# Fourteen constant matmuls between routing and experts, and the down matmuls of block 6 ahead of the up matmuls of block 8

## The chip, the cores and the metric

One core of one Trainium2 chip runs the whole program. The metric is the device time in microseconds of one execution. TensorE (PE in the profile) does the matmuls, VectorE (DVE) and ScalarE (ACT) the elementwise work, GpSimd (POOL) some elementwise work and the indirect transfers, and SyncE (SP) issues nearly all other transfers. A profile is one execution taken by the hardware profiler; the times of the runs are taken without it.

## What is computed

The input `x` is 1024 tokens of 128 features, the context 6404 rows of 128. Cut to what matters:

```python
def xattn(c, q):                      # c = layernorm(x), q = context
    s = (c @ w_c + b_c)[:, :, None] + (q @ w_q + b_q)[:, None, :] + einsum('bcd,bqd,d->bcq', c, q, w_cq) + b_cq
    c2q = softmax(s, axis=2) @ q
    q2c = softmax(max(s, axis=2)) @ c
    return concat([c, c2q, c * c2q, c * q2c]) @ W_l.T + b_l
def ffn(x):                           # 8 experts, H 128, F 512, top 1
    expert_id = argmax(x @ wr + br)
    y_e = gelu(x @ w1[e] + b1[e]) @ w2[e] + b2[e]
    return y of the chosen expert
x = x + xattn(layernorm(x), ctx)
x = x + ffn(layernorm(x))
```

## The kernel before, in words

The first part (to about 171 us of the profiled span) is the attention: eight tiles of 128 tokens against seven groups of 1024 context rows, in f16 pairs of a high and a low part. The change lies behind it.

Then comes routing. On TensorE: `turn_x2` transposes the normalised rows of tiles 0 to 6, `router` makes their scores, `linear_a(3)` and `linear_c(2)` finish the attention's linear layer of tile 7, and the matmuls of L1210 to L1217 count ranks within each expert once VectorE has the one-hot choices (`chosen_ready`). VectorE turns the counts into positions (`pos_ready`, L955), finishes the layernorm of tile 7 (L760), and L1221 transposes that tile. ScalarE and VectorE split the transpose into high and low parts (L690, L964, `x7T_low`), for which the first expert matmuls wait.

The experts work in blocks. `NBLK` is 22: blocks 0 to 7 (`b < E`) put tile 7 through each of the eight experts with a mask; blocks 8 to 21 are dispatched blocks, up to 128 rows each that chose the same expert. For every block `up(b)` is 16 matmuls of 128 columns (L1265 to L1268, four per piece of the hidden layer), ScalarE takes the gelu twice (L708, L709), VectorE makes the low part of the hidden values (L983, `h_low`), and `down(b)` is four matmuls of 256 columns (L1279), one with the bias (L1282), then behind a wait for `h_low` four of 128 columns (L1285). VectorE finishes the block in two halves (L992 or L996, then L1006 or L1008, `y_ready`). Buffers for hidden values and results are a ring of three blocks. TensorE's order is written out by hand: in iteration `b` it runs `up(b + 2)` and then `down(b)`.

Dispatched rows take a way through device memory. After `pos_ready` GpSimd scatters the rows of seven tiles into `rows_by_expert` (L600, seven indirect transfers). SyncE waits for all of them (`rows_sent`) and then loads the rows of batches of 3, 4, 4 and 3 blocks (L447, `rows_landed`), in one queue with the fourteen copies of each block's weights (L442, `fetch`, 512 KB each). TensorE's `turn(g)` (L1239) transposes batch g in float32; ScalarE (L698) and VectorE (L975, `xT_low`) split it into two f16 parts. `turn(0)` stands at the head of iteration 6, `turn(1)` in iteration 6 behind `up(8)`, `turn(2)` in iteration 10 and `turn(3)` in iteration 14. `up(8)` waits for `xT_low` of batch 0. Blocks 8 to 21 leave by one indirect scatter each on GpSimd (L606), in order, each behind its `y_ready`. With the last of them landed the program ends.

`psS` is three PSUM tiles of two banks each. `psS[2][:, 0:512]` holds the transposes of `turn_a(0)` and of `turn_x2`'s first group earlier, and `up(2)` writes it later. `ones` is a float32 tile of ones.

Of the kernel before, what the change touches and what calls it, by code (L numbers as in the profile page):

```python
# [24 lines left out]
F16 = mybir.dt.float16  # L25
# [5 lines left out]
P = 128  # L31


def build(nc, x, ctxT, w3, b3, wlT, b_l, wr, br, w1, b1, w2, b2, out):
    N, D = x.shape
    Q = ctxT.shape[1]
    E, _, F = w1.shape
    T = N // P
    QT = -(-Q // P)
    QP = QT * P  # L40
    FC = F // P
    CH = 512
# [32 lines left out]
    def tiles(e):  # L75

        return range(e * TW, min((e + 1) * TW, QT))

    es = ExitStack()
    with es:  # L80
        def sb(name, shape, dt=F32):
            return es.enter_context(nc.sbuf_tensor(name, shape, dt))
# [24 lines left out]
        ones = sb("ones", [P, P])  # L107
# [88 lines left out]
        psS = [es.enter_context(nc.psum_tensor(f"psS{i}", [P, GR], F32)) for i in range(BANKS)]  # L196
# [126 lines left out]
        def rows_of(n):  # L323

            k = len(tiles(n))
            buf = qT[:, n, :, :] if n < NG - 1 else qTend[:, :, :]
            return buf.rearrange("p a w -> p (a w)"), qn[:, 2 * n * TW:2 * n * TW + 2 * k, :]
# [38 lines left out]
        def _(sp):  # L366
# [18 lines left out]
            def transpose(t, e):  # L385

                wait_low(sp, t, e)
                if t > 0:
                    sp.wait_ge(pv_done, (t - 1) * NG + e + 1)
                src, _, _, dst = piece(t, e)  # L390
                sp.dma_start_transpose(dst, src).then_inc(pT_landed[e], 16)
# [636 lines left out]
        def _(pe):  # L1028
# [30 lines left out]
            def weighted(t, e):  # L1059

                pe.wait_ge(pT_landed[e], 16 * (t + 1))
                if t == 0:
                    pe.wait_ge(qn_landed[e], 16)
                if t == 0 and e == 0:
                    pe.wait_ge(cT_ready, 1)
                if t == 1 and e == 0:
                    pe.wait_ge(row_term_ready, 1)
                if e == 0 and t > 1:
                    pe.wait_ge(o_out, t - 1)
                n, acc = len(tiles(e)), psA[t % 2]  # L1070
                both = rows_of(e)[1].rearrange("p (a j) d -> p a j d", a=2)
                for i, j in enumerate(tiles(e)):
                    nc.tensor.matmul(acc[:, 0:2 * D].rearrange("p (a d) -> p a d", a=2), PT[:, 2 * e * TW + i, :],  # L1073
                                     both[:, :, i, :], start=(j == 0), stop=False, skip_group_check=True)
                    last = nc.tensor.matmul(acc[:, 0:D], PT[:, 2 * e * TW + n + i, :], both[:, 0, i, :],  # L1075
                                            start=False, stop=(j == QT - 1), skip_group_check=True)
                last.then_inc(pv_done, 1)
# [43 lines left out]
            def linear_a(g):  # L1121

                t0, t1 = TURNS[g]
                pe.wait_ge(caT_ready, g + 1)
                if g < 2:
                    pe.wait_ge(nM_ready, 1)
                pe.wait_ge(late_landed, 16 * NLATE)
                for t in range(t0, t1):
                    k = t // H if t < T - 1 else 2
                    dst = z_psum[k][:, (t - GROUPS[k][0]) * D:(t - GROUPS[k][0] + 1) * D]  # L1130
                    r = slice(t * P, (t + 1) * P)
                    nc.tensor.matmul(dst, aT[:, r], wl[:, 1, :], start=(t == GROUPS[k][0]), stop=False,
                                     skip_group_check=True)
                    nc.tensor.matmul(dst, caT[:, r], wl[:, 2, :], start=False, stop=False, skip_group_check=True)

            def linear_c(g):

                t0, t1 = GROUPS[g]
                pe.wait_ge(wc2_ready, 1)
                for t in range(t0, t1):  # L1140
                    last = nc.tensor.matmul(z_psum[g][:, (t - t0) * D:(t - t0 + 1) * D], cT[:, t * P:(t + 1) * P],
                                            wc2[:, :], start=False, stop=(t == t1 - 1), skip_group_check=True)
                last.then_inc(z_in_psum, 1)
# [26 lines left out]
            def mean_context():  # L1170

                pe.wait_ge(eb_ready, 1)
                for t in range(T):
# [2 lines left out]
                nc.tensor.matmul(psS[1][:, CH:CH + 1], ones[:, :], es1[:, :], start=True, stop=True)\  # L1176
                    .then_inc(q2c_in_psum, 1)

            weighted(T - 2, 2)
            pe.wait_ge(scores_out, T * NG)  # L1180
            turn_a(0)
# [19 lines left out]
            for e in range(2, NG):  # L1201
# [3 lines left out]
            router()  # L1205
            linear_a(3)
            linear_c(2)

            pe.wait_ge(chosen_ready, 1)
            nc.tensor.matmul(rank_psum, before[:, :], oneh[:, :, :].rearrange("p t e -> p (t e)"),  # L1210
                             start=True, stop=False, skip_group_check=True)
            for t in range(TA - 1):
                nc.tensor.matmul(rank_psum[:, (t + 1) * E:TA * E], ones16[:, :],
                                 oneh[:, t, :].unsqueeze(1).broadcast_to([P, TA - 1 - t, E]),
                                 start=False, stop=(t == TA - 2), skip_group_check=True)
            for t in range(TA):
                last = nc.tensor.matmul(count_psum, ones16[:, :], oneh[:, t, :], start=(t == 0), stop=(t == TA - 1))  # L1217
            last.then_inc(ranks_in_psum, 1)

            pe.wait_ge(x2n_ready, H + 1)  # L1220
            nc.tensor.transpose(x7T_psum, x2n[:, TA, :], idf[:, :]).then_inc(x7T_in_psum, 1)  # L1221
# [8 lines left out]
            def turn(g):  # L1230

                s0, s1 = BATCHES[g]
                pe.wait_ge(rows_landed[g], 16)
                if g == 0:
                    pe.wait_ge(mask_ready, 1)
                if g >= 2:
                    pe.wait_ge(xT_low, g - 1)
                for b in range(s0, s1):
                    last = nc.tensor.transpose(psXT[g % 2][:, (b - s0) * P:(b - s0 + 1) * P], rows[:, b, 0:D], idf[:, :])  # L1239
                last.then_inc(xT_in_psum, 1)  # L1240

            def weights(b):

                return wp[:, :, b * F:(b + 1) * F] if b < E else block_w(b - E)

            def bias_rows(b):

                return pick[:, b, :] if b < E else chosen[:, b - E:b - E + 1].broadcast_to([P, P])

            def up(b):  # L1250

                i, j = b % RING, b - E if b >= E else NB
                if b >= E:
                    g = [s0 <= j < s1 for s0, s1 in BATCHES].index(True)
                    pe.wait_ge(xT_low, g + 1)
                    pe.wait_ge(block_w_landed[j % WSLOTS], 16 * (j // WSLOTS + 1))
                    pe.wait_ge(chosen_rows, 1)
                else:
                    pe.wait_ge(x7T_low, 1)
                if b >= RING:  # L1260
                    pe.wait_ge(h_full, b - RING + 1)
                for f in range(FC):
                    dst = psH[i][:, f * P:(f + 1) * P]
                    w_h, w_l = (weights(b)[:, a, f * P:(f + 1) * P] for a in range(2))
                    nc.tensor.matmul(dst, w_h, xTp[:, 0, j, :], start=True, stop=False)  # L1265
                    nc.tensor.matmul(dst, w_h, xTp[:, 1, j, :], start=False, stop=False)
                    nc.tensor.matmul(dst, w_l, xTp[:, 0, j, :], start=False, stop=False)
                    last = nc.tensor.matmul(dst, b12[:, f * P:(f + 1) * P],  # L1268
                                            bias_rows(b), start=False, stop=True)
                last.then_inc(h_in_psum, 1)  # L1270

            def down(b):

                i = b % RING
                if b >= RING:
                    pe.wait_ge(y_ready, b - RING + 1)
                pe.wait_ge(h_high, b + 1)
                for f in range(FC):
                    nc.tensor.matmul(psY[i].rearrange("p (a d) -> p a d", a=2), hp[:, i, 0, f * P:(f + 1) * P],  # L1279
                                     weights(b)[:, 2:4, f * P:(f + 1) * P],  # L1280
                                     start=(f == 0), stop=False, skip_group_check=True)
                nc.tensor.matmul(psY[i][:, 0:D], bias_rows(b), b12[:, F:F + D], start=False, stop=False, skip_group_check=True)  # L1282
                pe.wait_ge(h_low, b + 1)
                for f in range(FC):
                    last = nc.tensor.matmul(psY[i][:, 0:D], hp[:, i, 1, f * P:(f + 1) * P],  # L1285
                                            weights(b)[:, 2, f * P:(f + 1) * P],
                                            start=False, stop=(f == FC - 1), skip_group_check=True)
                last.then_inc(y_in_psum, 1)
# [7 lines left out]
            for b in range(NBLK):  # L1296
                if b == E - 2:
                    turn(0)
                for g, (s0, _) in enumerate(BATCHES):
                    if g >= 2 and b == E + s0 - 5:  # L1300
                        turn(g)
                if b + 2 < NBLK:
                    up(b + 2)
                if b == E - 2:
                    turn(1)
                down(b)


# [29 lines left out]
```

## Time and profile before

| | us |
|---|---|
| three runs: lowest, median, highest | 236.48, 237.16, 238.58 |
| the profiled execution: its own time | 234.7 |
| its span, from the first to the last event of the trace | 233.0 |
| mean granted clock of TensorE, share of full | 0.937 |
| TensorE busy in the span | 200.8 (86%) |

All positions below are microseconds from the start of the span. The span is 1.7 us shorter than the execution's own time.

### The profile page before, as it was taken

What the parts mean: (1) busy time and instruction counts of PE and PEld (TensorE: products, weight loads), DVE (VectorE), ACT (ScalarE), POOL (GpSimd) and SP (SyncE); (2) the same over time, 40 slices, a digit from 0 to 9 for tenths busy, and PEclk for the clock granted to TensorE, in tenths of its full rate; (3) what the DMA queues carried; (4) which work ended last, traced back from release to release, by engine and by line L of the source; (5) the groups of instructions that cost most, each with busy time, mean ns of one, the idle gap of its engine ahead of it and who ended that gap; (6) DMA issues with size and microseconds to landing.
All of it is one profiled execution on the core that took longest, in us unless ns stands there. A gap on an engine that the chain in (4) does not pass through costs nothing.

```text
span 233.0 us, 5011 instructions
## 1 busy us (share of the span) xinstructions
PE 200.8 (86%) x1837; PEld 151.4 (65%) x1837; DVE 180.4 (77%) x395; ACT 157.9 (68%) x249; POOL 126.6 (54%) x177
## 2 busy tenths in 40 slices
PE   0289969999999999979989999899992899799970
PEld 0133436776866777746656777699981899789960
DVE  2999797697998997997995999957848437567770
ACT  2752899399399698699596799789332355766630
POOL 3695819708906808958608957655302730027783
PEclk9999985799999999999999999999996569999995
DMA  6999979979999999999989999989991559999100
GB/s 208 381 259 258 221 239 249 225 192 191 232 180 227 260 220 271 231 200 240 230 207 274 207 249 230 211 180 212 234 284 47 191 191 314 366 370 344 43 21 0
DMA packets 142958, 51.78 MB, mean 222 GB/s; under 512 B 121172, under 2 KB 140773, under 8 KB 142934
## 3 DMA queue, kind: packets, MB, share of 16 engines
q1 hardware_dynamic: 142000, 50.08, 92.8%
q0 software_dynamic: 784, 1.38, 1.7%
q8 instruction: 14, 0.23, 0.4%
q14 instruction: 10, 0.08, 0.1%
q10 hardware_dynamic: 150, 0.00, 0.0%
HBM read 10.74 MB, written 3.75 MB: 62 GB/s over the span
## 4 chain that ended last, share of the span: by engine, by line
PE 41%; DVE 23%; issue 13%; DMA 11%; POOL 6%; ACT 4%; SPq 1%; POOLq 0%; DVEq 0%; ACTq 0%
DMA PT<-Phl 9%; DVE S L798 6%; PE psX L1073 6%; PE psS L1055 5%; PE psS L1053 5%; PE psS L1054 5%; POOL out_x L606 5%; PE psO L1073 4%; DVE Phl L815 4%; PE psX L1075 3%; ACT S L649 3%; PE psO L1075 2%; PE psS L1279 2%; DMA S<-in_x 2%; PE psX L1084 2%
## 5 line engine op out<-in xcount | busy, mean ns | idle before, releaser
L649 ACT ACTIVATE S<-S,negb 128x1024 f32<-128x1024 f32 x48 | 55.0, 1145 | 17.5 <-DVE negb L806 17.5
L798 DVE TENSOR_SCALAR_CACHE_REDUCE S<-psS 128x1024 f32<-128x1024 f32 x48 | 58.2, 1216 | 9.9 <-PE psS L1055 9.8
L815 DVE TENSOR_TENSOR Phl<-S,Phl 128x1024 f16<-128x1024 f32 x38 | 51.5, 1354 | 5.3 <-ACT Phl L664 5.2
L531 POOL TENSOR_TENSOR Phl<-S,Phl 128x256 f16<-128x256 f32 x40 | 26.4, 691 | 52.2 <-ACT Phl L664 52.2
L664 ACT CAST Phl<-S 128x1024 f16<-128x1024 f32 x48 | 50.2, 1045 | 5.6 <-DMA PT<-Phl 4.2
L1053 PE MATMUL psS<-qT,gh 128*128 128x512 f16 x96 | 37.6, 392 | 5.6 <-DVE gl L776 3.0
L1073 PE MATMUL psO<-qn,PT 128*128 128x256 f16 x204 | 37.7, 279 | 0.7 <-DMA PT<-Phl 0.7
L1073 PE MATMUL psX<-qn,PT 128*128 128x256 f16 x204 | 36.4, 273 | 2.0 <-DMA PT<-Phl 2.0
L1055 PE MATMUL psS<-qT,gl 128*128 128x512 f16 x96 | 37.7, 393 | 0.0
L1054 PE MATMUL psS<-qT,gh 128*128 128x512 f16 x96 | 37.7, 393 | 0.0
L1075 PE MATMUL psO<-qn,PT 128*128 128x128 f16 x204 | 36.2, 223 | 0.0
L1075 PE MATMUL psX<-qn,PT 128*128 128x128 f16 x204 | 35.0, 219 | 0.0
L606 POOL DMA_INDIRECT out_x<-stageT,S x14 | 16.8, 1198 | 24.3 <-DVE stageT L1006 18.5
L1073 PEld LDWEIGHTS psO<-qn,PT 128*128 128x128 f16 x204 | 20.4, 100 | 6.5 <-DMA PT<-Phl 1.9
L1073 PEld LDWEIGHTS psX<-qn,PT 128*128 128x128 f16 x204 | 20.0, 98 | 6.7 <-DMA PT<-Phl 2.7
L708 ACT ACTIVATE Phl<-psS 128x512 f16<-128x512 f32 x22 | 13.1, 597 | 15.4 <-PE psS L1268 8.7
L1075 PEld LDWEIGHTS psO<-qn,PT 128*128 128x128 f16 x204 | 20.4, 100 | 2.2 <-issue 0.3
L1075 PEld LDWEIGHTS psX<-qn,PT 128*128 128x128 f16 x204 | 20.0, 98 | 2.1
L1053 PEld LDWEIGHTS psS<-qT,gh 128*128 128x128 f16 x96 | 9.8, 102 | 14.7 <-DVE S L798 3.5
L1055 PEld LDWEIGHTS psS<-qT,gl 128*128 128x128 f16 x96 | 9.7, 101 | 12.1 <-issue 1.4
L983 DVE TENSOR_TENSOR Phl<-Phl 128x512 f16<-128x512 f32 x22 | 15.0, 681 | 2.4 <-issue 2.4
L572 POOL TENSOR_TENSOR wp<-stageT,wp 128x256 f16<-128x256 f32 x16 | 15.2, 982 | 0.3
(239 smaller groups left out, 426.3 us busy)
## 6 DMA issues: line engine op xcount, KB each, us to landing
PT<-wp SPq DMA_DIRECT2D x8, 512.0 KB, 6.0
stageT<-in_ctxT SPq DMA_DIRECT2D x6, 512.0 KB, 7.3
qn<-wp SPq DMA_DIRECT2D x6, 512.0 KB, 6.5
wp<-in_w SPq DMA_DIRECT2D x4, 512.0 KB, 4.8
stageT<-in_w SPq DMA_DIRECT2D x4, 512.0 KB, 4.8
rows_by_expert<-stageT SPq DMA_DIRECT2D x4, 385.5 KB, 5.3
PT<-Phl SPq DMA_TRANSPOSE x48, 4.2
S<-rows_by_expert SPq DMA_DIRECT2D x2, 258.0 KB, 5.9
```

Source lines behind the costliest of these rows:

```text
L531: last = nc.gpsimd.tensor_tensor(lo[:, r], slot(t, e)[:, r], hi[:, r], ALU.subtract)
L572: last = nc.gpsimd.tensor_tensor(parts[:, 1, at + a:at + a + CHUNK], src[:, a:a + CHUNK], parts[:, 0, at + a:at + a + CHUNK], ALU.subtract)
L606: pool.indirect_dma_start(out=out, out_offset=bass.IndirectOffsetOnAxis(ap=rows[:, b, 2 * D:ROW].bitcast(I32), axis=0), in_=yf[:, b, :], i ...
L649: nc.scalar.activation(slot(t, e), slot(t, e), ACT.Exp, bias=negb[:, t:t + 1], accum_out=Lp[:, t * NG + e:t * NG + e + 1]).then_inc(exp_do ...
L664: nc.scalar.copy(hi, slot(t, e)).then_inc(high_done, 1)
L798: nc.vector.tensor_scalar(out=into, in0=bank(u, n)[:, 0:into.shape[1]], scalar1=1.0 / GS, scalar2=None, op0=ALU.mult, op1=ALU.max, accum_o ...
L815: nc.vector.tensor_tensor(lo, slot(t, e), hi, ALU.subtract).then_inc(low_done, 1)
L1053: nc.tensor.matmul(dst, g_h, hi, start=True, stop=False)
L1054: nc.tensor.matmul(dst, g_h, lo, start=False, stop=False)
L1055: last = nc.tensor.matmul(dst, g_l, hi, start=False, stop=True)
L1073: nc.tensor.matmul(acc[:, 0:2 * D].rearrange("p (a d) -> p a d", a=2), PT[:, 2 * e * TW + i, :], both[:, :, i, :], start=(j == 0), stop=Fa ...
L1075: last = nc.tensor.matmul(acc[:, 0:D], PT[:, 2 * e * TW + n + i, :], both[:, 0, i, :], start=False, stop=(j == QT - 1), skip_group_check=True)
```

## The change

Two edits, both in TensorE's program. The first adds `fill(n)`, which issues n f16 matmuls of 128 rows by 512 columns from the constant tile `ones` into `psS[2][:, 0:512]`, where nobody reads them. They signal nothing and wait for nothing of their own. Two stand behind `linear_c(2)`, ahead of the wait for `chosen_ready`; twelve behind the rank and count matmuls, ahead of the wait for tile 7's normalised rows. The second edit moves `down(6)` in iteration 6 from behind `up(8)` and `turn(1)` to right behind `turn(0)`.

```diff
+            filler = ones[:, :].bitcast(F16)
+            def fill(n):
+                for _ in range(n):
+                    nc.tensor.matmul(psS[2][:, 0:CH], filler[:, 0:P],
+                                     filler.unsqueeze(1).broadcast_to([P, 2, 2 * P]), start=True, stop=True)
...
             router()
             linear_a(3)
             linear_c(2)
+            fill(2)
 
             pe.wait_ge(chosen_ready, 1)
...
             last.then_inc(ranks_in_psum, 1)
+            fill(12)
 
             pe.wait_ge(x2n_ready, H + 1)
...
                 if b == E - 2:
                     turn(0)
+                    down(b)
                 for g, (s0, _) in enumerate(BATCHES):
...
                 if b == E - 2:
                     turn(1)
-                down(b)
+                else:
+                    down(b)
```

## Rows read from the trace of the kernel before

**Rows 1.** The page, 40 equal slices of the span (5.8 us each), in tenths.

```profile
PEclk9999985799999999999999999999996569999995
DMA  6999979979999999999989999989991559999100
```

**Rows 2.** Chain that ended last from 165 us on: start, us, what.

```profile
by line: issue 21.6%; POOL out_x L606 14.9%; DMA PT<-Phl 5.5%; PE psS L1279 5.5%; PE psS L1265 4.7%; PE psS L1266 4.2%; PE psS L1267 4.2%; PE psS L1268 4.1%; PE psS L1285 2.8%; PE psS L1166 2.4%; PE psX L1073 1.9%; DVE S L975 1.5%; DVE stag
...
205.91 0.29 DVE stageT L1006
...
207.03 0.99 POOL out_x L606
...
227.37 0.08 POOL out_x L606
...
228.66 0.98 POOL out_x L606
```

**Rows 3.** Busy time of each engine by stage; behind them clock, DMA share, GB/s.

```profile
175.17:176.50 1.33, 0.51 (x14) 0.42 (x14) 1.16 (x7) 0.00 (x0) 0.00 (x0) 1.00 0.49 118
176.50:181.44 4.94, 0.48 (x1) 0.21 (x2) 3.67 (x19) 2.06 (x5) 1.79 (x2) 0.50 0.08 30
181.44:190.16 8.72, 8.72 (x73) 8.25 (x74) 2.61 (x12) 3.04 (x7) 5.56 (x6) 0.50 0.60 212
```

**Rows 4.** TensorE's timeline around routing: start, us, instruction, [idle before, releaser].

```profile
175.78 0.20 PE L1210 MATMUL psS<-S,before 128*128 128x56 f16 x1 [0.61 <-DVE S L939]
...
180.12 0.48 PE L1221 MATMUL psO<-idf,qT 128*128 128x128 f32 x1 [3.84 <-DVE qT L760]
...
181.44 0.27 PE L1265 MATMUL psS<-S,wp 128*128 128x128 f16 x1 [0.84 <-DVE S L964]
```

**Rows 5.** TensorE's timeline early: 512-column f16 matmuls at either clock.

```profile
14.24 0.63 PE L1054 MATMUL psS<-qT,gh 128*128 128x512 f16 x1
14.67 0.63 PE L1055 MATMUL psS<-qT,gl 128*128 128x512 f16 x1
...
17.52 0.38 PE L1053 MATMUL psS<-qT,gh 128*128 128x512 f16 x1
17.74 0.38 PE L1054 MATMUL psS<-qT,gh 128*128 128x512 f16 x1
```

**Rows 6.** TensorE's timeline at the switch to dispatched blocks.

```profile
197.58 0.50 PE L1239 MATMUL psX<-idf,S 128*128 128x128 f32 x3
199.51 0.23 PE L1265 MATMUL psS<-S,PT 128*128 128x128 f16 x1 [1.44 <-DVE S L975]
...
200.42 0.60 PE L1239 MATMUL psO<-idf,S 128*128 128x128 f32 x4
200.86 0.60 PE L1279 MATMUL psS<-wp,Phl 128*128 128x256 f16 x4
...
201.57 0.22 PE L1265 MATMUL psS<-S,PT 128*128 128x128 f16 x1
...
206.87 0.61 PE L1239 MATMUL psX<-idf,S 128*128 128x128 f32 x4
```

**Rows 7.** VectorE's timeline at the switch, the low part of block 6's hidden values.

```profile
198.05 0.68 DVE L983 TENSOR_TENSOR Phl<-Phl 128x512 f16<-128x512 f32 x1
```

**Rows 8.** SyncE's queue: issues of the row loads of batches 0 and 1, 2, 3.

```profile
190.01 0.90 SPq L447 DMA_DIRECT2D S<-rows_by_expert  x2
...
196.55 1.30 SPq L447 DMA_DIRECT2D S<-rows_by_expert  x1
...
202.07 0.97 SPq L447 DMA_DIRECT2D S<-rows_by_expert  x1
```

**Rows 9.** Last figure, us to landing: batch 0, batch 2; last row: all weight copies (L442).

```profile
S<-rows_by_expert SPq DMA_DIRECT2D x1, 192.0 KB, 2.6
...
S<-rows_by_expert SPq DMA_DIRECT2D x1, 256.0 KB, 6.3
...
DMA to landing us min/median/max: 5.6/6.1/6.9
```

## The prediction

> **What bounds the kernel now.** I read the page first. In its forty slices TensorE's clock is at full speed except in two stretches, and the second lies at slices 31 to 33 (175 to 192 us), between routing and the experts; the transfers are light in its first slices and at nine tenths from slice 34 to slice 37, that is to 215.5 us [rows 1]. The attention ahead of 171 us isn't touched, so I ask only what sets the time from there on. The chain of waits from 165 us has as its largest piece by name the output scatters on GpSimd, 14.9% of its stretch, and then TensorE's matmuls of the blocks [rows 2]. The scatters look like the bound and aren't one: the first starts 1.1 us after VectorE began to write its block (205.91, 207.03), and the last two are 1.29 us apart (227.37, 228.66) [rows 2], while a block costs TensorE 0.89 us for 16 up matmuls (199.51 to 200.42, less 0.02 of start) and 0.71 us for the down matmuls (200.86 to 201.57) [rows 6], together 1.60 us. A GpSimd that needs 1.29 follows a TensorE that gives a block every 1.60. So the end is the time of the first dispatched block plus thirteen blocks of TensorE, and whatever lets TensorE come there earlier shortens the kernel, until a transfer is late.
>
> The table by stage shows where TensorE loses [rows 3]. From 176.50 to 181.44 it is nearly idle and its clock drops to 0.50 (1.2 GHz). From 181.44 to 190.16 it is busy all of the 8.72 us, still at 0.50. Before 176.50 it was at 1.00, with only 0.51 us of work in the last 1.33.
>
> **The twelve fills behind the counts.** Their place is the idle time of 3.84 us ahead of the transpose at 180.12, and they end before it if they are fast. A 512-column matmul starts 0.22 us after the one before at the full clock (17.52, 17.74) and 0.43 us at the half clock (14.24, 14.67) [rows 5]. Twelve take 2.6 us at full: issued from about 176.3 on, they end near 178.9, 1.2 us before the transpose. They touch no queue but TensorE's, no transfer, and a bank that nobody reads then. Their own cost is nothing as long as that idle time covers them; all at the half clock they take 5.2 us, end at 181.5 and hold the transpose up by 1.4 us.
>
> What they may bring: if the clock is still at 1.00 at 181.44, the 8.72 us shrink by the ratio of 0.22 to 0.43, to 4.5 us. That saves 4.2 us. The bounds are nothing (the clock falls all the same) and 4.4 us (exactly half). I take 4.2, since the clock is at 1.00 when they begin and full work always kept it there in this trace, and what is left idle between 178.9 and 181.44 is 2.5 us with a transpose in it, half of what is there now. ScalarE and VectorE follow: in the stretch they are busy 3.0 and 2.6 of 8.7 us [rows 3], so both fit into half of it.
>
> The Trainium skill has a rule that speaks against so large a gain: "TensorE: Matmul & The Clock Gate", Part 1, "What's actually happening", says the ramp penalty is under 1% of a typical kernel's span, so at most 2.3 us here. By that rule the fills bring 2.3 us. The row disagrees: 8.72 us of solid work at half clock are 1.8% of the span in lost time, and the row decides.
>
> **The two fills ahead of the ranks.** TensorE sits idle for 0.61 us before 175.78, waiting for VectorE's one-hot [rows 4]. Two fills at full take 0.44 us and fit. At the half clock they take 0.86, push the ranks by 0.25 us, and behind these stand VectorE's positions, the GpSimd scatters and every row load. The row of that stage says 1.00 [rows 3], so I take 0, with 0.25 us of loss as the other bound.
>
> **Moving the down matmuls of block 6.** Today TensorE ends `turn(0)` near 197.9 and is held 1.44 us until VectorE has split batch 0 (199.51) [rows 6]. Then come `up(8)`, `turn(1)` at 200.42, and only then `down(6)` for 0.71 us. Its low half needs the hidden values' low part, made from 198.05 to 198.73 [rows 7]. Moved into the wait, its first five matmuls take 0.49 us at once, the rest 0.22 us from 198.73, and it is through at 199.0, before 199.51. So the whole 0.71 us leaves the path. VectorE keeps its order: finishing block 6 still stands behind its split of batch 0, and its input is merely earlier. `turn(1)` and `up(9)` come 0.71 us earlier; their inputs (batch 1's rows, ScalarE's full gelu of block 6) are there, as the next section shows for the rows. Bounds: 0, if the moved work runs into the split's end, and 0.75. I take 0.7.
>
> **What is late next.** Both together bring TensorE 4.9 us forward. SyncE's queue doesn't move: its first row load is issued at 190.01 behind the scatters, and those hang on VectorE's positions, which the change doesn't touch. So each transfer has to be set against its new need.
> - Batch 0: issued 190.01, lands 2.6 us later, 192.6 [rows 8, 9]. Needed at 197.58 - 4.2 = 193.4. In time by 0.8.
> - Batch 1: issued in the same pair near 190.4; even with 5 us it is there at 195.4, and is needed behind `up(8)` at 200.42 - 4.2 = 196.2.
> - Batch 2: issued 196.55, lands 6.3 us later, 202.85 [rows 8, 9]. `turn(2)` stands at 206.87 today [rows 6] and would come at 206.87 - 4.9 = 201.97. It has to wait 0.9 us. This is the term that the two edits don't show by themselves.
> - Batch 3: issued 202.07, with the slowest 6.9 us of rows 9 there at 209.0. `turn(3)` is four blocks behind `turn(2)`: 202.85 + 0.44 + 4 x 1.60 = 209.7. In time by 0.7.
> - Weights: all copies are through when the transfers fall from nine tenths, by 215.5 [rows 1]; the last up matmuls begin nine blocks behind `turn(2)`, at 202.85 + 0.44 + 9 x 1.60 = 217.7.
> - The first three output scatters now fall into the saturated stretch. Each writes at most 128 rows of 512 bytes, an eighth of a weight copy; three of them delay the later loads by a fraction of a microsecond, inside the 0.7.
>
> **Sum.** 4.2 + 0.7 - 0.9 = 4.0 us less. The profiled execution's 234.7 us (span 233.0 and 1.7 around it) becomes 230.7. The runs' median stands 2.5 us above the profiled execution; I take the difference over to it: 237.2 - 4.0 = 233.2 us. A measurement of this kernel can tell about 1% from no change, 2.4 us.
>
> **Rivals.**
> 1. *The clock is only partly kept.* For: it falls and rises at moments that have nothing to do with the kernel's stages (it rose at 190.16 in the middle of a block [rows 3]), so in another execution it may fall before the fills are through. If six of the twelve run at the half clock, these cost 6 x 0.21 = 1.3 us more, of which the 1.2 us ahead of the transpose hide nearly all; if the clock falls behind them, part of the 8.72 us stays slow. Priced at 3.4 us left slow: 1.7 us lost, of which 0.9 was to be lost at `turn(2)` anyway. Gain 3.2, time 234.0. Against: fill work is dense. The Trainium skill says in the same section that the gate's check runs freely and isn't tied to the kernel's start, so that the cold part differs from run to run; the profile of one execution can't show that. By its 1% rule the sum would be 2.3 + 0.7 = 3.0 and 234.2 us, with no wait left at `turn(2)`.
> 2. *The fills don't hold the clock* (constant data, nothing reads it, the idle rest is too long). Then they cost nothing and bring nothing, the 8.72 us stay, and only the second edit is left: 0.7 us, 236.5. Against: every dense stretch in this trace kept 1.00.
> 3. *The transfers are late by more than I count.* `turn(2)` already waits, so every microsecond that batch 2 lands later than in this profile is lost whole. At 1.5 us later, or with a weight copy late for an up matmul, the gain is 2.5, 234.7. For: the transfer engines are saturated exactly there. Against: nothing that the change does before 202 us adds to them.
> 4. *Slower: the fills run cold and in the way.* If the clock drops before the fills begin (TensorE had only 0.51 us of work in the 1.33 before 176.50) and stays at half through them, the transpose of tile 7 waits for the twelfth. Each costs 0.43 us; from the seventh on they pass the cover of 3.84 us, less what they start late, and at twelve the delay is 1.4 us. The ranks are late by 0.25. With the clock low through the experts' start nothing is won back, the second edit gives 0.7, and the time is 1.0 us longer: 238.2. It decides from nine cold fills on, which is where the cover ends (9 x 0.43 = 3.87). Against: 5 us of solid matmuls should raise the clock as the solid work after 181.44 does, 8.7 us after its start at the latest.
>
> **Chances.** Forecast (gain about 4) 0.58; rival 1 0.20; rival 2 0.08; rival 3 0.09; rival 4 0.05. The range: above, rivals 3 and part of 2, with the bounds of the terms and the median's own unrest of about a microsecond, 235.7. Below, no wait at `turn(2)` and a cold stretch that was longer in the timed runs than in the profile, 4.9 + 0.6: 231.7. Faster by over 1%: the forecast, most of rival 1 and half of rival 3, 0.79. Within 1%: rival 2, the rest of 1 and 3, and most of rival 4, 0.17. Slower by over 1%: 0.04.
>
> **What would show it.** In the profile after: the clock 1.00 from the fills through the first up matmuls; the first up matmul still near 181.4; the twelve fills 0.22 us apart and ended by 179; `turn(0)` near 193.4; `down(6)` done before the first matmul of `up(8)`; a new idle time of about 0.9 us before `turn(2)`, put down to the row load; the last scatter near 224.7. I'm wrong if the first up matmul is later than 181.9, if the clock's cold stretch is still there, or if an up matmul of a dispatched block waits for its weights.

## The result, and the profile after

| | before | after |
|---|---|---|
| median of 20 runs each, us | 235.94 | 238.06 |
| lowest, highest | 233.61, 238.58 | 235.42, 240.62 |
| profiled execution, span | 234.7, 233.0 | 236.09, 234.3 |
| mean granted clock | 0.937 | 0.958 |

The ratio is 1.0076 with a 95% interval of [1.004, 1.0112]: the change costs 1.8 us, where 4.0 us of gain were forecast. The ratio leaves out executions more than 1.5% above the fastest of the same kernel, which the table's medians include. TensorE's mean clock is higher and the kernel slower.

The page of the kernel after: TensorE's clock and the transfers in forty slices (it answers to [rows 1]).

```profile
PEclk9999985799999999999999999999999979999995
DMA  6999979999999999999999999989990749997100
```

The three low slices between routing and the experts (31 to 33 before) have gone, but for a 7 in slice 33, behind the place where the fills were to help. TensorE's timeline (start, us, instruction, idle before and its releaser) shows the fills at work; it answers to [rows 4].

```profile
175.40 0.59 PE L1184 MATMUL psS<-ones 128*128 128x512 f16 x2
176.18 0.20 PE L1219 MATMUL psS<-S,before 128*128 128x56 f16 x1 [0.18 <-DVE S L939]
176.54 2.75 PE L1184 MATMUL psS<-ones 128*128 128x512 f16 x12
180.53 0.33 PE L1231 MATMUL psO<-idf,qT 128*128 128x128 f32 x1 [1.24 <-DVE qT L760]
181.70 0.22 PE L1275 MATMUL psS<-S,wp 128*128 128x128 f16 x1 [0.84 <-DVE S L964]
...
186.96 0.22 PE L1276 MATMUL psS<-S,wp 128*128 128x128 f16 x1 [0.99 <-issue]
187.70 0.22 PE L1275 MATMUL psS<-S,wp 128*128 128x128 f16 x1 [0.41 <-issue]
188.40 0.22 PE L1276 MATMUL psS<-S,wp 128*128 128x128 f16 x1 [0.49 <-issue]
189.83 0.22 PE L1276 MATMUL psS<-S,wp 128*128 128x128 f16 x1 [1.04 <-issue]
```

Up to 181.70 all is as forecast. Then come gaps that weren't there, put down to no other engine. The table by stage says what they did to the pace (columns as in [rows 3]; the first two rows answer to the last two there, the third is the stretch behind them).

```profile
176.50:181.44 4.94, 3.12 (x21) 1.25 (x17) 3.75 (x20) 1.95 (x4) 1.39 (x2) 1.00 0.01 3
181.44:190.16 8.72, 5.52 (x76) 4.77 (x77) 2.50 (x12) 2.64 (x6) 5.58 (x6) 1.00 0.64 228
190.16:194.50 4.34, 4.15 (x39) 3.64 (x37) 2.32 (x6) 2.94 (x6) 0.00 (x0) 0.61 0.64 191
```

The same three stretches of the kernel before, of which the third isn't in [rows 3], so it is shown here:

```profile
190.16:194.50 4.34, 4.34 (x69) 4.21 (x68) 3.02 (x8) 3.20 (x7) 0.00 (x0) 1.00 0.79 235
```

In the 8.72 us TensorE recorded 76 matmuls at the full clock against 73 at the half clock [rows 3]. The doubled clock moved the work on by three matmuls. In the next 4.34 us it recorded 39 against 69, since the clock now falls there (0.61). That is 27 matmuls less in all, at 0.056 us each (0.89 us for 16 up matmuls) 1.5 us: and `turn(0)` comes 17.57 us behind the first up matmul (199.27 - 181.70) where it came 16.14 behind it before (197.58 - 181.44), 1.43 later.

What TensorE waits for is seen on the engine that it feeds. ScalarE's timeline, kernel after: the first gelu of blocks 0, 1 and 2.

```profile
183.26 0.60 ACT L708 ACTIVATE Phl<-psS 128x512 f16<-128x512 f32 x1 [1.41 <-PE psS L1278]
...
188.42 0.60 ACT L708 ACTIVATE Phl<-psS 128x512 f16<-128x512 f32 x1 [4.07 <-remote]
...
189.95 0.60 ACT L708 ACTIVATE Phl<-psS 128x512 f16<-128x512 f32 x1 [0.45 <-remote]
```

The same engine, kernel before, block 2:

```profile
189.45 0.60 ACT L708 ACTIVATE Phl<-psS 128x512 f16<-128x512 f32 x1 [2.25 <-remote]
```

"Remote" is how the profile names a releaser that it can't find: `up(1)`, for which the gelu at 188.42 waits, has its last matmul recorded from 184.08 to 184.30. ScalarE, free from 184.35 on, got to know of it 4 us later, and VectorE likewise (its row at 190.06 in `after` has 4.10 of idle time, remote). The kernel before shows it too, with a wait that ends at 189.45, and in that profile TensorE lost nothing by it: at the half clock it was busy through all of the 8.72 us and of the 4.34 behind them. GpSimd's timeline shows what runs through all of it, the scatters of the rows (the first and the last of seven):

```profile
179.75 1.21 POOL L600 DMA_INDIRECT rows_by_expert<-qT,S  x1 [9.22 <-DVE S L955]
...
187.59 0.96 POOL L600 DMA_INDIRECT rows_by_expert<-qT,S  x1 [0.30 <-issue]
```

My theory from here on: while GpSimd issues its seven scatters, what TensorE has finished reaches the other engines late. The rivals: the weight copies of the first blocks, which share the stretch; the bytes of the scatters rather than their issue; and nothing of the kind, only the fills' own effect. One more falls by this trace: TensorE starved of its own program. The transfers that load instructions have queues of their own on the profile's page (q8 and q14, 24 packets over the span), and from 174 to 189 us neither of them moved a packet in `after`.

Four figures of each profile tell the runs apart, all read from rows: ScalarE's idle time before its work for block 1; `turn(0)` less the first up matmul; the first output scatter less `turn(0)`; the last output scatter less the first. A fifth pair stands between them: the matmuls that TensorE recorded in the 8.72 us from its first up matmul, and the granted clock there.

| run (chip) | ScalarE, block 1 | matmuls, clock | to turn(0) | to first out | to last out |
|---|---|---|---|---|---|
| before | 1.68 | 73, 0.50 | 16.14 | 9.45 | 21.63 |
| after | 4.07 remote | 76, 1.00 | 17.57 | 8.74 | 22.02 |
| e1 fills only (11) | 4.06 remote | 76, 0.93 | 17.01 | 9.45 | 21.92 |
| e2 order only (11) | 1.68 | 82, 0.69 | 15.90 | 8.75 | 23.34 |
| e3 copies late (11) | 4.05 remote | 79, 1.00 | 17.59 | 8.74 | 21.90 |
| e4 one scatter (11) | 0.46 | 134, 1.00 | 12.08 | 8.75 | 23.45 |
| e5 one scatter, no fills (4) | 1.68 | 80, 0.57 | 15.58 | 8.75 | 21.63 |
| e7 narrow rows (4) | 0.46 | 134, 1.00 | 12.08 | 8.74 | 22.71 |
| e9 before, four more scatters (4) | 1.68 | 96, 0.68 | 14.60 | 9.52 | 21.56 |
| f4 as e9 (4) | 1.68 | 77, 0.53 | 15.90 | 9.51 | 21.57 |
| f1 after again (4) | 0.46 | 134, 1.00 | 12.09 | 8.74 | 25.65 |
| g1 after again (5) | 3.96 remote | 80, 1.00 | 17.37 | 8.74 | 21.90 |
| g2 narrow rows (5) | 5.65 remote | 74, 1.00 | 17.81 | 8.73 | 21.91 |
| g4 order only (5) | 2.27 | 81, 0.65 | 15.96 | 8.74 | 21.63 |
| h1 rows early (0) | 0.46 | 134, 1.00 | 12.08 | 8.75 | 22.55 |
| h2 order only (0) | 1.68 | 92, 0.66 | 14.83 | 8.74 | 21.62 |

The first up matmul itself lies between 180.1 and 185.1 us over all the profiles, with the same code ahead of it; this is why I read distances and not positions. Without fills the clock rises at a different point of the experts' start in each profile (0.50 to 0.69 over the same 8.72 us), so that a distance is best compared with one of the same kernel or of the same chip.

### The profile page after: what moved, and what is told of

It is laid out like the page before. It is cut to its first block, busy times and chain, and to the rows that moved or that the text cites. A ratio compares the mean times of both kernels' runs of the same rounds, so it can differ in the third digit from the quotient of the medians.

```text
span 234.3 us, 5039 instructions
## 1 busy us (share of the span) xinstructions
PE 202.7 (86%) x1851; PEld 149.7 (64%) x1851; DVE 180.5 (77%) x395; ACT 157.5 (67%) x249; POOL 125.0 (53%) x177
## 4 chain that ended last, share of the span: by engine, by line
PE 36%; DVE 24%; issue 14%; DMA 9%; ACT 8%; POOL 5%; another core or an unknown queue 2%; DVEq 0%; POOLq 0%; ACTq 0%
DMA PT<-Phl 7%; DVE S L798 6%; PE psO L1073 5%; ACT S L649 5%; PE psS L1053 4%; DVE Phl L815 4%; PE psS L1055 4%; PE psS L1054 4%; POOL out_x L606 4%; PE psX L1073 4%; PE psO L1075 2%; ACT Phl L664 2%; PE psX L1075 2%; DMA S<-in_x 2%
## 5 line engine op out<-in xcount | busy, mean ns | idle before, releaser
L815 DVE TENSOR_TENSOR Phl<-S,Phl 128x1024 f16<-128x1024 f32 x38 | 50.8, 1337 | 5.6 <-ACT Phl L664 5.5
L606 POOL DMA_INDIRECT out_x<-stageT,S x14 | 15.9, 1134 | 26.6 <-DVE stageT L1006 22.0
L572 POOL TENSOR_TENSOR wp<-wp 128x256 f16<-128x256 f32 x16 | 15.3, 987 | 0.3
```

The lines of the kernel that those rows point to most:

```text
L572: last = nc.gpsimd.tensor_tensor(parts[:, 1, at + a:at + a + CHUNK], src[:, a:a + CHUNK], parts[:, 0, at + a:at + a + CHUNK], ALU.subtract)
L606: pool.indirect_dma_start(out=out, out_offset=bass.IndirectOffsetOnAxis(ap=rows[:, b, 2 * D:ROW].bitcast(I32), axis=0), in_=yf[:, b, :], i ...
L815: nc.vector.tensor_tensor(lo, slot(t, e), hi, ALU.subtract).then_inc(low_done, 1)
```

## The experiments

Diffs are against the kernel after unless they say otherwise.

### Each edit alone

```diff
 # e1_fills_only: the order of before
                 if b == E - 2:
                     turn(0)
-                    down(b)
...
-                else:
-                    down(b)
+                down(b)
 # e2_order_only, g4_order_only, h2_order_only: no fills
-            fill(2)
...
-            fill(12)
```

> The fills alone, the down matmuls of block 6 back in their old place. In the profile after, TensorE ran warm from 181.7 and then stood for about 4 us (185.8 to 189.9), and ScalarE got the signal of block 1's up matmuls at 188.4 where the last of them is recorded at 184.4. Theory A (something outside TensorE holds its results back until about 190, so a faster clock only lengthens the wait, and the wait lets the clock fall behind it): as slow as the full change or slower, 0 to 3 us above before, with the idle time at 186 to 190 and a cold stretch behind it. Theory B (the fills do what was forecast and the moved down matmuls are what costs): 4 us faster than before.

> No fills, only the moved down matmuls of block 6. Theory A: the 0.7 us of the forecast, 0.3 to 1.0 us faster than before, since the edit lies behind the hold-up. Theory B: slower than before by 1 to 3 us, the loss of the full change.

Fills only: 237.28 against 235.75, ratio 1.0045 [1.0, 1.009]. Order only: 234.47, 0.9926 [0.9882, 0.997]. So the loss comes with the fills, though the interval of e1 begins at no loss at all. The moved `down(6)` takes 0.7 us off the way from `turn(0)` to the first output scatter (9.45 to 8.75), as forecast, and with it alone the hold-up is there as before (ScalarE idle 2.37 us, remote, ahead of block 2). It isn't free in e2, though it was in the profile of the kernel before. The same kernel on chip 0 (h2), at nearly the same clock, has no such wait; first e2, then h2, from their first up matmuls:

```profile
180.13:188.85 8.72, 8.16 (x82) 7.58 (x82) 2.50 (x12) 2.92 (x7) 5.56 (x6) 0.69 0.60 212
```

```profile
181.61:190.33 8.72, 8.72 (x92) 8.41 (x93) 3.34 (x14) 4.26 (x9) 5.55 (x6) 0.66 0.60 212
```

Ten matmuls fewer, and `turn(0)` 15.90 us behind the first up matmul instead of 14.83; g4 on chip 5 has 81 matmuls and 15.96. Where the clock comes back early, the hold-up costs about 1.1 us without any fills, by these three profiles. From the first output scatter to the last e2 takes 23.34 us instead of h2's 21.62, and there too results arrive late: VectorE is idle for 1.58 us twice, ahead of its rows at 211.15 and 215.20, where h2 shows 0.52 to 0.96. So e2's profile shows no gain from the edit, and its ratio owes something to chance. I ran it twice more.

> The moved down matmuls of block 6 alone, as e2, which was 0.3 to 1.2% faster than before on the first chip. If its gain is the 0.7 us worked out from the trace: 0.2 to 0.6% faster. If it came from chance in the first run: no difference.

> Only the moved down matmuls of block 6, once more. From turn(0) to the first output scatter 8.74 us instead of 9.45, whatever the signals do. The theory says 0.7 us less, ratio 0.997 (0.993 to 1.000). The rival, that the 0.7 us are taken back by transfers or by output scatters that come earlier, says 1.000 to 1.002.

On chip 5 it gave 234.55 in 12 runs, ratio 0.9996 [0.995, 1.0042], on chip 0 234.63 in 12 runs, 0.9997 [0.9961, 1.0033]. The 0.71 us stand in every profile; in the time they are inside the unrest of the runs. 0.3% would be 0.7 us, and the two later intervals hold both that and nothing.

### Whose hold-up it is

```diff
 # e3_copies_late: SyncE fetches the first blocks' weights behind the scatters
-            for b in range(FIRST):
-                fetch(b)
...
+            for b in range(FIRST):
+                fetch(b)
 # e4_one_scatter: one scatter of seven
-            sp.wait_ge(rows_sent, 16 * TA)
+            sp.wait_ge(rows_sent, 16)
+            sp.wait_ge(y_in_psum, 2)
...
-            for t in range(TA):
+            for t in range(1):
```

> The full change, and the weight copies of dispatched blocks 0 and 1 issued behind the row loads of batches 0 and 1 instead of near 183. They then don't run beside the up matmuls of blocks 1 and 2 (184.3 to 188.1 before). If these copies hold TensorE up: no idle time at 186 to 190, turn(0) near 193.5, and the time falls, though batch 2's rows come 2.8 us later. If the row scatters or something else holds it up: TensorE's idle time ends near 190 as before, and the time rises by up to 2 us.

> The full change, with one row scatter instead of seven (six tiles' rows are never dispatched, their outputs are left out), and the row loads waiting for block 1's down matmuls instead, so that they don't start early. The two weight copies stay at 183. If the scatters hold TensorE up: no idle time at 186 to 190, ScalarE takes block 1 near 184.4, block 1's down matmuls end near 187. If the copies hold it up: the idle time is still there until 188.

e4 leaves out the rows of six tiles. Both ran on chip 11 with e1. Without the copies beside it the idle time is 4.05, ratio 1.0086 [1.0039, 1.0133]: the copies fall out as a cause. With one scatter it is gone from this place; here is the first gelu of block 1 in either, e3 first, then e4.

```profile
190.48 0.60 ACT L708 ACTIVATE Phl<-psS 128x512 f16<-128x512 f32 x1 [4.05 <-remote]
```

```profile
184.38 0.60 ACT L709 ACTIVATE Phl<-psS 128x512 f16<-128x512 f32 x1 [0.46 <-PE psS L1279]
```

And e4's table by stage, the 8.72 us from its first up matmul:

```profile
181.75:190.47 8.72, 8.72 (x134) 8.41 (x135) 5.58 (x19) 5.84 (x12) 0.00 (x0) 1.00 0.41 138
```

134 matmuls instead of 76, at the same clock, and 231.57 us in its single execution. This is what the fills were to bring: `turn(0)` is 4.06 us nearer to the first up matmul than in the profile of before (16.14 - 12.08). GpSimd has nothing to do in that stretch (0.00).

The late results come back in the same profile, once GpSimd issues the output scatters close together (208.33 and 209.94, each 0.30 us behind the one before). ScalarE:

```profile
210.61 0.60 ACT L709 ACTIVATE Phl<-psS 128x512 f16<-128x512 f32 x1 [2.29 <-remote]
```

The up matmuls that it waits for are recorded as ended at 208.74, and VectorE's row at 211.38 has 2.40 of idle time, remote. From the first output scatter to the last, e4 takes 23.45 us.

The next four went to chip 4. e5 is e4 without fills; e6 holds all seven scatters back until block 2 is done; e7 sends 16 columns of each row into another tensor (the dispatched rows are left out); e9 is the kernel before with four more scatters into a tensor that nobody reads.

```diff
 # e6_scatters_late, f3 and g3
+            pool.wait_ge(y_in_psum, 3)
             for t in range(TA):
 # e7_narrow, f2 and g2
-                pool.indirect_dma_start(out=xs, ...
-                                        in_=pay[:, t, :], in_offset=None)
+                pool.indirect_dma_start(out=xn, ...
+                                        in_=pay[:, t, 0:16], in_offset=None)
```

> As e4_one_scatter (one row scatter instead of seven, the rows of six tiles are left out), but without the fills. It is the control for e4, in which the way from the first up matmul to turn(0) took 12.08 us. If the fills' worth is real once the scatters are out of the way: the cold stretch is back and the way is 16.1 us as before, 4 us more than in e4. If taking the scatters out was the whole gain of e4: near 12.1 us here too.

> The full change, with GpSimd waiting for block 2's down matmuls before it starts the seven row scatters. If it is the scatters that hold TensorE's results back: blocks 0 to 2 run warm and unhindered (ScalarE takes block 1 near 184.4 and block 2 near 185.4), and the late signals and idle times of TensorE reappear 1 to 9 us behind the new start of the scatters, near 189 to 197. If the hold-up belongs to that place of TensorE's program (its instructions, the first blocks): it stays at 184 to 190. The time rises by the delay of the rows, some 8 to 10 us, in either case.

> The full change, with the seven row scatters cut from 257 values per row to 16 and sent to a tensor of its own (the dispatched rows are left out). Same number of rows, a sixteenth of the bytes. If the bytes on their way to device memory hold TensorE up: no late signal, ScalarE takes block 1 near 184.5. If it is GpSimd's making of the 128 row transfers: the same 4.0 us wait of ScalarE for block 1.

> The kernel before with four more row scatters (to a tensor that nobody reads) behind the seven, on GpSimd from 188.8 to 193.9; the row loads wait only for the first seven. If scatters hold TensorE up wherever it runs at full clock: blocks 3 to 6, 1.6 us each there before, stall until about 194 to 195, and turn(0) comes 2 to 4 us later than 16.1 us after the first up matmul. If the hold-up is peculiar to the first blocks: no change of that distance.

One execution of each: e5 234.86, e6 241.95, e7 231.88, e9 234.83, the kernel before 233.39. e6 and e7 showed 0.45 and 0.46 us of idle time, so either could have been taken for a cure. But these runs lacked the kernel after on the same chip, and so I ran it there, with f2, f3 and f4 as copies of e7, e6 and e9.

> The changed kernel itself once more, beside the three below on the same chip, since the last four ran on another chip than the first four. There none of e6, e7 and e9 showed late signals of TensorE, scatters or not. If the hold-up belongs to the kernel: ScalarE again waits 4.0 us for block 1 (4.07, 4.06 and 4.05 us in the three traces with fills and seven scatters so far), turn(0) comes 17.0 to 17.6 us after the first up matmul, and the time is 0.5 to 1% above before. If it belongs to the chip: neither, and 12 to 13 us.

> As e7_narrow: the full change with the seven row scatters cut to 16 values per row and sent to a tensor of their own (the dispatched rows are left out). If the bytes of the scatters hold TensorE up, then beside f1 with a 4.0 us wait of ScalarE for block 1 this one has 0.5 us, and turn(0) 12.1 us after the first up matmul. If the making of the transfers on GpSimd does it: 4.0 us here too.

> As e6_scatters_late: the seven row scatters wait for block 2's down matmuls. If scatters hold TensorE up wherever they run: late signals behind 189.5. If they do so only beside the first blocks: none, as in e6, also where f1 shows them.

> As e9_again: the kernel before with four more row scatters behind the seven. If scatters hold TensorE up wherever it runs at full clock, blocks 3 to 6 stall here where f1 shows the hold-up: turn(0) 2 to 4 us later than 16.1 us after the first up matmul. If not, 14.5 to 16.2 us.

f1, the unchanged kernel after on chip 4, has no hold-up either: 0.46 us, with all seven scatters. From its first up matmul:

```profile
183.29:192.01 8.72, 8.72 (x134) 8.41 (x135) 5.78 (x19) 5.84 (x12) 6.11 (x6) 1.00 0.62 220
```

GpSimd is busy for 6.11 us of it and TensorE loses nothing. Chip 4 doesn't show the thing in any of its profiles, and e5 to e9 and f2 to f4 tell nothing about its cause. What they do say: without the fills e5, e9 and f4 need 15.58, 14.60 and 15.90 us to `turn(0)`, with them e7 and f1 need 12.08 and 12.09. So on this chip the fills bring 2.5 to 3.8 us up to there, by how long the clock would have stayed low, and not quite the 4.2 that I forecast. f2 took 233.85, f3 244.01, f4 235.92 in one execution each. Three of them I ran again on a chip that does show it.

> The changed kernel itself, to see which kind of run this is. If its up matmuls are held up: ScalarE waits 4.0 us for block 1, turn(0) 17 to 17.6 us after the first up matmul, 0.4 to 0.8% slower than before. If not: 0.5 us and 12.1 us, and the time within 0.5% of before, since the wait of turn(2) for batch 2's rows and the clock that falls in it take the 4.8 us back.

> The seven row scatters cut to 16 values per row (the dispatched rows are left out). Tells something only beside a g1 with the hold-up: 0.5 us wait of ScalarE for block 1 if the bytes of the scatters are the cause, 4.0 us if GpSimd's making of the transfers is.

> The seven row scatters wait for block 2's down matmuls. Beside a g1 with the hold-up: if scatters hold TensorE up wherever they run, ScalarE's waits for blocks 5 to 7 (0.52 us in e6) grow to 1 to 4 us; if the hold-up is tied to the first blocks, its wait for block 1 is 4.0 us with no scatter there.

On chip 5, g1 (the kernel after) is held for 3.96 us in its profile, an execution of 239.15 us. Its times don't bear out the 0.4 to 0.8% that I expected: 237.37 against 236.32 at the median, ratio 0.9994 [0.9948, 1.004]. That is no different from f1's on chip 4, so the split between the chips rests on the profiles and not on the times. g2 writes a tiny part of the bytes, and its block 1 is held longer (ScalarE):

```profile
192.39 0.60 ACT L709 ACTIVATE Phl<-psS 128x512 f16<-128x512 f32 x1 [5.65 <-remote]
```

So it isn't the bytes, as far as one profile says. In g3 the scatters begin at 191.63. Until then ScalarE waits 0.46 us for block 1 and TensorE records 134 matmuls in 8.72 us, like f1; behind it the releases come late. g3's ScalarE and then its VectorE:

```profile
191.65 0.60 ACT L709 ACTIVATE Phl<-psS 128x512 f16<-128x512 f32 x1 [0.52 <-PE psS L1279]
193.73 0.60 ACT L709 ACTIVATE Phl<-psS 128x512 f16<-128x512 f32 x1 [1.00 <-PE psS L1279]
```

```profile
195.20 0.35 DVE L997 SCALAR_TENSOR_TENSOR stageT<-psS,S,stageT 128x128 f32<-128x128 f32 x1 [1.62 <-PE psS L1296]
198.88 0.35 DVE L997 SCALAR_TENSOR_TENSOR stageT<-psS,S,stageT 128x128 f32<-128x128 f32 x1 [2.47 <-remote]
```

The same kernel on chip 4 (f3) has 0.52 in front of each of these ScalarE rows and 0.40 in front of each of these VectorE rows, also with its scatters running. The hold-up moved with the scatters. As versions, e6, f3 and g3 (245.49) lose because the row loads stand behind the scatters: TensorE waits 8.38 us for rows before `turn(0)` in g3.

### The late rows

f1 gained 4.05 us to `turn(0)` and 0.71 behind it, and its time is only 0.9975 [0.9928, 1.0023] of before (235.25 against 235.03 at the median). TensorE's timeline says where it went:

```profile
206.28 0.92 PE L1249 MATMUL psX<-idf,S 128*128 128x128 f32 x4 [2.16 <-DMA S<-rows_by_expert]
```

The chain has the load that released it, from its issue:

```profile
198.73 7.51 DMA S<-rows_by_expert
```

and the table by stage, the clock behind the wait:

```profile
203.29:207.29 4.00, 1.84 (x18) 1.56 (x16) 1.09 (x3) 1.14 (x3) 1.98 (x2) 0.90 1.11 370
207.29:211.29 4.00, 4.00 (x45) 3.72 (x43) 1.06 (x4) 1.79 (x4) 0.00 (x0) 0.67 1.09 366
```

`turn(2)` stands 2.16 us for batch 2, and the matmuls behind it run at a fallen clock: 25.65 us from the first to the last output scatter instead of 21.63. 4.02 of 4.76 us are given back. The last run moves that load ahead of the weight copies of two blocks.

```diff
 # h1_rows_early: in SyncE's program
+            block_rows(2, 0, D, rows_landed)
...                                # fetch(4) and fetch(5)
-            block_rows(2, 0, D, rows_landed)
```

> The whole change, and behind turn(0) the loads of batch 2's rows are issued ahead of the weight copies of blocks 4 and 5 instead of behind them. If TensorE's signals are held up beside the scatters (ScalarE idle for about 4 us before its work for block 1), turn(0) comes 17 to 18 us behind the first up matmul, turn(2) had no wait, and nothing is gained by it: ratio 1.00 to 1.01, and a weight copy that now lands later may cost an up matmul a fraction of a us. If they are not (wait of 0.5 us), turn(0) comes 12.1 us behind the first up matmul, and the wait of 2.16 us before turn(2) with the low clock behind it goes: 25.65 us from the first to the last output scatter become 22 to 23.5, and the kernel is 2 to 4 us faster than before, 0.98 to 0.99.

Chip 0 shows no hold-up (0.46 us). 232.91 against 235.19, ratio 0.9891 [0.983, 0.9952] over 4 runs: the fastest version of the study against its own runs of before. h1's TensorE at `turn(2)` and `turn(3)`:

```profile
204.48 0.61 PE L1249 MATMUL psX<-idf,S 128*128 128x128 f32 x4
...
212.24 0.55 PE L1249 MATMUL psO<-idf,S 128*128 128x128 f32 x3 [0.38 <-DMA S<-rows_by_expert]
```

No wait at `turn(2)`, 0.38 us at `turn(3)`, and 22.55 us to the last scatter. Against the profile of before that is 4.06 + 0.70 - 0.92 = 3.84 us, near the forecast's 4.0. But that profile has a longer stretch at the half clock than h2, from chip 0 like h1. With h2's way to `turn(0)` the fills bring 14.83 - 12.08 = 2.75, and the sum is 2.75 + 0.70 - 0.92 = 2.53 us, which is what the ratio says of the times (1.09% of 235.19, 2.6 us). On a chip that holds TensorE's results this version wasn't run.

## Why the prediction was wrong

**Held.** The fills' own cost: nothing; they are 0.22 us apart and leave 1.24 us before the transpose. The ranks still wait, 0.18 us, so the two fills fit. The clock: 1.00 from the fills into the experts. The first up matmul: 181.70, under the 181.9 at which I said I would be wrong. The moved `down(6)`: 0.7 forecast, 0.71 measured. Batch 0 and 1 in time. Rivals 2 and 4 fell with the clock. Rival 1 came half true: in five of the thirteen profiles with fills (e1, e4, e6, g3, h1) the clock was at 0.50 through part of them (in e1 from 175.94 to 179.35), but it was back at 1.00 before the first up matmul in each, and the cover of 3.84 us hid what the cold fills cost.

**The step that failed** is the 4.2 us: "if the clock is still at 1.00 at 181.44, the 8.72 us shrink by the ratio of 0.22 to 0.43, to 4.5 us", with "ScalarE and VectorE follow", for which I added up their busy time. I took a stretch in which TensorE was busy 8.72 of 8.72 us for one that only its clock limits. There was a second limit with the same end, the hold-up that lets go at about 190, and faster matmuls run into it. What in the chip makes this limit stays open. With it the stretch kept its length (3 matmuls more of 73), and behind it the clock fell, which my account had as a thing of the past: 1.43 us lost where 4.2 were to be gained. My bounds for the term, nothing and 4.4, left this side out. Where the hold-up is absent from this place (f1, h1, e4), the term measures 4.05 to 4.06 against the profile of before, and 2.5 to 3.8 against the profiles without fills of the same chip (e5, e9, f4, h2): the length of the cold stretch that it is to save differs from execution to execution, and I took it from one.

The row that speaks of it was in the trace of before and I didn't ask for it: ScalarE idle for 2.25 us, released by something unnamed, in the middle of a stretch in which TensorE feeds it without pause, and 1.7 us behind the recorded end of the matmuls that it waited for. Busy shares of ScalarE and VectorE can't show that; the releasers can.

**Mis-sized, and covered up.** I forecast 0.9 us of wait at `turn(2)`. In the kernel after it is nothing, because everything came late; in f1 it is 2.16 us (the load took 7.5 us to land, against 6.3 in rows 9), plus the clock that falls behind it. That is rival 3, with a price above the one I gave. So even on chip 4 the forecast's 4.0 us came to 0.7 in the profile and to 0.6, not clear of nothing, in the times.

**Whether slower.** I gave slower by over 1% a chance of 0.04, yet the only rival that was slower, the cold fills of rival 4, was priced at 1.0 us, which is 0.4%. Its working contradicts itself, too: cold fills pass the cover of 3.84 us from the ninth on (9 x 0.43 = 3.87), not from the seventh. The time came out 0.76% longer, with an interval from 0.4 to 1.12, above my range, and by a way that no rival named.

The Trainium skill's rule on the ramp ("TensorE: Matmul & The Clock Gate", Part 1, "What's actually happening": under 1% of a typical kernel's span) doesn't fit here: it is said beside measurements of a kernel's start, and this stretch lies in the middle. Where nothing else holds TensorE, the cold stretch costs 2.5 to 4.1 us, 1.1 to 1.7% of 233.0; where something does, taking it away brought nothing.

## What to carry to other kernels

Before a slow clock is priced as lost time, read the releasers of the engines that TensorE feeds in that stretch: a wait put down to nobody, or to a matmul that ended long before, is a second limit with the same end, and a faster TensorE only idles in front of it and may find its clock lowered behind it. Where an engine is brought forward by several microseconds, bring forward the loads it will need next in the same change. And run the unchanged kernel on each chip on which an experiment runs: ten of my eighteen met a chip where the effect isn't there, and what I first took for the fills' full worth was partly the difference between two executions.

## What the runs showed of the hardware

- Beside seven back-to-back indirect scatters of 128 rows, GpSimd busy for 0.96 us of every 1.27, results of TensorE reached ScalarE and VectorE about 4 us late (4.07, 4.06, 4.05, 3.96; 5.65 with short rows) and TensorE then stood still in pieces of 0.4 to 1.2 us, put down to issue. Whether its signals are late, or the matmuls themselves, whose ends are modelled, these traces don't tell apart. TensorE starts again in steps of 0.70 to 0.74 us or twice that (186.96, 187.70, 188.40, 189.83 in `after`; 190.23, 191.66, 193.08 in g1), and not in the scatters' step of 1.27.
- It depends on the chip or something that goes with it: seen in the first measurement and on chips 11 and 5, absent in every profile of chip 4 and in both of chip 0. (No wait in ScalarE's or VectorE's timelines from 179 to 231 us is put down to "remote" in their ten profiles.) Each version has one profile, and the times of the chips don't show the split. Why stays open. So does what in the scatters does it: not their bytes (g2), and not the weight copies beside them (e3). That one scatter doesn't do it rests on one profile (e4), that it moves with them on one (g3). On chips 11 and 5 it comes back beside the output scatters: 2.29 us at ScalarE and 2.40 at VectorE in e4, 2.43 at VectorE in g3 (at 233.25).
- Stalls of TensorE can lower its clock afterwards, also in work that is dense again: 0.61 at 190.16 to 194.50 behind the hold-up, 0.67 behind the wait of 2.16 us. In f1 the second loss was about as large as the wait itself (4.02 us in all). They needn't: behind a wait of 1.87 us at the same `turn(2)` f2 stayed at 1.00 (205.47 to 209.47).
- The cold stretch ahead of the experts differs between executions, with the same matmuls in it: without fills the clock over the 8.72 us from the first up matmul was 0.50, 0.53, 0.57, 0.65, 0.66, 0.68 and 0.69 in seven profiles. With fills it was at 1.00 at the first up matmul in all thirteen.
